# Sixteen-head attention: a cap applied by factors, work moved between four engines, a new slot table

## The reference

```
x = x + L0_attn(layernorm(x));  x = x + L0_moe(layernorm(x))      # before the stage of interest
q, k, v = split(layernorm(x) @ in_proj.T + in_proj_bias)           # 16 heads of 8
bias    = minimum((i - j) * slope[h], 8.0)                         # i query, j key; slope[h] = 2 ** (-0.5 (h+1))
scores  = q @ k.T * 8 ** -0.5 + bias
out     = softmax(scores) @ v                                      # per head
x = x + (out @ out_proj.T + out_proj_bias)
x = x + L1_ffn(layernorm(x))                                       # top-1 of 8 experts, after the stage
```

## Time and profile before

| | us |
|---|---|
| median of 3 runs | 988.6 |
| lowest, highest | 988.32, 989.9 |
| profiled execution | 988.53 |
| its span in the trace | 986.5 |

### The profile page before, as it was taken

The page is one execution under the profiler, slowest core; times in us unless marked ns, Lnnn a source line. Parts: engine busy times, 40 slices in busy tenths (PEclk is TensorE's granted clock), DMA queues, the critical chain, the costliest instruction groups (busy, mean ns, idle before and its releaser), DMA issues.

```text
span 986.5 us, 19021 instructions
## 1 busy us (share of the span) xinstructions
PE 783.2 (79%) x5641; PEld 564.8 (57%) x5641; DVE 549.3 (56%) x2190; ACT 395.9 (40%) x947; POOL 357.9 (36%) x543
## 2 busy tenths in 40 slices
PE   0798479999999999952489999999999982038894
PEld 0676355555666677742246676667666651028883
DVE  4688573233322332333588989898987714026672
ACT  0456121222212322210036666766676661025562
POOL 5000517777850134433222423242322102744552
PEclk9999668999999999986569999999999995559997
DMA  9970001111100132303654444444443014111110
GB/s 250 155 221 0 0 1 36 40 41 41 44 0 14 52 112 78 96 30 90 128 106 95 90 108 93 102 83 106 95 85 67 3 45 155 54 53 55 50 50 14
DMA packets 75114, 72.44 MB, mean 73 GB/s; under 512 B 8125, under 2 KB 65680, under 8 KB 72732
## 3 DMA queue, kind: packets, MB, share of 16 engines
q1 hardware_dynamic: 69436, 60.38, 27.3%
q0 software_dynamic: 5600, 11.12, 3.5%
HBM read 43.71 MB, written 27.33 MB: 72 GB/s over the span
## 4 chain that ended last, share of the span: by engine, by line
PE 52%; DVE 18%; issue 12%; DMA 5%; POOL 5%; ACT 3%; DVEq 2%; SPq 2%; POOLq 0%; ACTq 0%
PE bank L1475 10%; PE bank L1476 9%; DVE rt L1065 6%; PE bank L1498 6%; PE bank L1527 4%; PE bank L1617 3%; PE bank L1569 3%; POOL sorted_rows L766 3%; PE bank L1604 3%; PE bank L1599 2%; DMA arena<-arena 2%; SPq L548 1%; DVEq L1180 1%; PE bank L1435 1%; PE bank L1707 1%
## 5 line engine op out<-in xcount | busy, mean ns | idle before, releaser
L1065 DVE CUSTOM_DVE_ANT_0 rt<-bank,alibi 128x256 f32<-128x256 f32 x512 | 192.9, 419 | 44.4 <-PE bank L1569 37.5
L973 DVE TENSOR_TENSOR arena<-arena,bank 128x512 f32<-128x512 f32 (+1 forms) x128 | 75.0, 587 | 187.8 <-ACT arena L1253 187.8
L1280 ACT ACTIVATE arena<-bank 128x512 f32<-128x512 f32 x256 | 150.6, 598 | 55.4 <-PE bank L1604 49.5
L1253 ACT ACTIVATE arena<-bank 128x512 f32<-128x512 f32 (+1 forms) x128 | 66.1, 517 | 202.9 <-PE bank L1476 202.9
L1569 PE MATMUL bank<-arena 72*128 72x256 bf16 x512 | 104.7, 289 | 26.6 <-DMA arena<-qk_parts 13.4
L1599 PE MATMUL bank<-arena 81*128 81x256 bf16 x512 | 117.0, 274 | 8.3 <-ACT arena L1280 4.7
L1475 PE MATMUL bank<-arena 128*128 128x320 f32 (+2 forms) x256 | 115.7, 534 | 7.5 <-DVE arena L973 7.5
L1476 PE MATMUL bank<-arena 128*128 128x320 f32 (+2 forms) x256 | 111.9, 519 | 0.0
L1604 PE MATMUL bank<-arena,ident_b 128*128 128x256 bf16 (+8 forms) x544 | 80.2, 243 | 0.0
L1569 PEld LDWEIGHTS bank<-arena 72*128 72x128 bf16 x512 | 39.0, 102 | 69.4 <-DVE arena L1065 42.8
L1475 PEld LDWEIGHTS bank<-arena 128*128 128x128 f32 x256 | 42.8, 193 | 53.5 <-DVE arena L973 41.1
(11 more groups left out here) (242 smaller groups left out, 1402.9 us busy)
## 6 DMA issues: line engine op xcount, KB each, us to landing
arena<-qk_parts SPq DMA_DIRECT2D x48, 192.0 KB
arena<-qk_parts SPq DMA_DIRECT2D x144, 64.0 KB
qk_parts<-arena SPq DMA_DIRECT2D x16, 384.0 KB, 2.8
back_rows<-empty_row SPq DMA_DIRECT2D x1, 4096.0 KB, 37.8
arena<-back_rows SPq DMA_DIRECT2D x16, 256.0 KB, 3.8
arena<-in_w SPq DMA_DIRECT2D x2, 2048.0 KB, 10.9
xg_rows<-empty_row SPq DMA_DIRECT2D x1, 2580.0 KB, 38.5
arena<-xg_rows SPq DMA_DIRECT2D x8, 322.5 KB, 4.0
```

The costliest lines, as they stand in the source:

```text
L973: nc.vector.tensor_tensor(out, sil[:, k, 0:out.shape[1]], bank[4 + k][:, 0:out.shape[1]], ALU.mult).then_inc(hid_done, 1)
L1065: last = nc.vector.tensor_tensor_reduce(biased[n % 2 * QT + u], bank[n % 2][:, SEQ * u:SEQ * u + SEQ], alibi[:, h, P * (1 - u):P * (1 - u) ...
L1253: nc.scalar.activation(sil[:, k, 0:width], bank[2 + k][:, 0:width], ACT.Silu).then_inc(sil_done, 1)
L1280: nc.scalar.activation(prT3[:, n % (2 * HG)].rearrange("p k t -> p (k t)"), bank[2 + n % 2][:], ACT.Exp).then_inc(exp3_done, 1)
```

## The change

Heads 2 to 8 lose their cap matmuls. Only heads 0 and 1 (`FULL = 2`) keep the bias as matmuls on PE. For heads 2 to 8 the scores hold the uncapped bias, and after the exponential POOL multiplies the columns where the cap bites by exp(8 - slope * distance) (`apply_factor`); the factor table is made once. `weigh` waits for these products (`factored`), is split over two slots (`WEIGH_0`, `WEIGH_1`) and stands three slots later, with a ring of 12 heads for `prT3` and of 5 batches for `v3`. The third norm is applied by ACT (two instructions) instead of DVE, from a shift and a scale that POOL works out in four steps instead of one. ACT also copies the values, without bias; the value bias is multiplied by the output weights once, and added to the output bias. ACT issues the DMA of the maxima. The offsets of nearly all steps are new, and the projection of q and k stands one slot behind that of the values.

```diff
-FULL = 4
+FULL = 2
+PR = 3 * HG
+VRING = 5
-COMBINE_0, COMBINE_1, STATS, VARIANCE, NORM, TURN, HT, QKV, QK_COPY, VALUES = -41, -40, -39, -38, -33, -30, -29, -26, -25, -19
+COMBINE_0, COMBINE_1, STATS, VARIANCE, ROOT, NORM_0, NORM_1, OUTPUT_BIAS = -42, -41, -38, -37, -36, -34, -33, -29
+TURN, HT, VALUE, QK, Q_COPY, K_COPY, PARTS_QK, VALUES = -32, -31, -27, -26, -25, -24, -23, -21
+SPLIT_MAX_0, SPLIT_MAX_1, TURN_MAX, COPY_MAX, SEND_MAX = NH + 1, NH + 2, NH + 4, NH + 5, NH + 6
+FACTOR, WEIGH_0, WEIGH_1, KEEP = EXP_LAG + 2, EXP_LAG + 6, EXP_LAG + 7, EXP_LAG + 8
...
# SP
-        def send_max(c):
-            wait_apart(sp, (max_rows_done, c + 1))
-            sp.dma_start(qs[MROW:KALL, c % RING], max_rows[0:PARTS * NH, c % 2]).then_inc(max_in[c % 2], 16)
...
# POOL
+        def apply_factor(n):
+            c, h = divmod(n, NH)
+            pool.wait_ge(exp3_done, n + 1)
+            if n == FULL:
+                pool.wait_ge(factor_set, 1)
+            for k in range(QT):
+                first = capped_from(h, k)
+                if first < SEQ:
+                    pr = prT3[:, n % PR, k, first:SEQ]
+                    last = nc.gpsimd.tensor_tensor(pr, pr, factor[:, h - FULL, first - P * k:SEQ - P * k], ALU.mult)
+            last.then_inc(factored, 1)
...
# DVE
-            nc.vector.tensor_scalar(mv[:, p, :, 2], mv[:, p, :, 1], LN_EPS, None, ALU.add).then_inc(var3_done, 1)
-        def norm3(c):
-                last = nc.vector.tensor_scalar(h3[:, c % 2, u, :], x[:, 2 * c + u, :], mv[:, c % 2, u, 0:1], rstd3[:, c % 2, u:u + 1],
-        def values(c):
-                last = nc.vector.tensor_tensor(v3[:, c % RING, u, :, 0:HD], bank[6][:, SEQ + D * u:SEQ + D * u + D].rearrange("p (h d) -> p h d", d=HD),
...
# ACT
+        def normalise(c, u):
+            last = nc.scalar.activation(h3[:, c % 2, u, :], x[:, QT * c + u, :], ACT.Identity, scale=norm3[:, c % 2, u, 1:2],
+                                        bias=norm3[:, c % 2, u, 0:1])
+        def values(c):
+                last = nc.scalar.activation(v3[:, c % VRING, u, :, 0:HD],
+        def send_max(c):
+            wait_apart(act, (max_rows_done, c + 1))
+            act.dma_start(qs[MROW:KALL, c % RING], max_rows[0:PARTS * NH, c % 2]).then_inc(max_in[c % 2], 16)
...
# PE
-        def weigh(g):
+        def weigh(g, u):
+            if u == 0:
+                pe.wait_ge(exp3_done, HG * (g + 1))
+                if k * HG < CLAMPED:
+                    pe.wait_ge(factored, factors_to(HG * g + HG - 1))
```

More of the change, by code:

```diff
@@ L82, with capped_from, factors_to @@
 SLOPE_PARTS = [bf16_parts(s) for s in SLOPES]
[L83 to L89, removed]
+BIAS_PARTS = [len([v for v in SLOPE_PARTS[h] if v]) for h in range(FULL)]
+STRIP = [sum(BIAS_PARTS[:h]) for h in range(FULL)]
+FACTORS = CLAMPED - FULL
+def capped_from(h, k):
+    return min((P * k + int(MAX_BIAS / SLOPES[h]) + 1) // 2 * 2, SEQ)
+def factors_to(n):
+    c, h = divmod(n, NH)
+    return FACTORS * c + min(max(h + 1 - FULL, 0), FACTORS)
 def batch_at(slot, offset):
@@ L284, in _build @@
     strip_a = carve([P, sum(BIAS_PARTS[:FULL]), SEQ + P], BF16)
[L285 to L288, removed]
+    factor = carve([P, FACTORS, SEQ])
     q_row = carve([P, SEQ], BF16)
@@ L1292, in turned, with copy_q @@
             if c >= 1:
-                act.wait_ge(v3_mm, c)
+                act.wait_ge(qk3_mm, c)
             nc.scalar.activation(hT3, bank[6][:, 0:SEQ], ACT.Copy).then_inc(hT3_done, 1)
-        def copy_qk(c):
+        def values(c):
+            act.wait_ge(v3_mm, c + 1)
+            if c >= VRING:
+                act.wait_ge(pv3_mm, NH // HG * (c - VRING + 1))
+            for u in range(QT):
+                last = nc.scalar.activation(v3[:, c % VRING, u, :, 0:HD],
+                                            bank[6][:, SEQ + D * u:SEQ + D * u + D].rearrange("p (h d) -> p h d", d=HD), ACT.Copy)
+            last.then_inc(v3_done, 1)
+        def copy_q(c):
             act.wait_ge(qk3_mm, c + 1)
@@ L1461, in _ @@
         pe.wait_ge(w3_in, 128)
+        pe.wait_ge(bv_done, 1)
+        nc.tensor.matmul(bank[7][:, P:2 * P], bv_cols[:], w_out[:], start=True, stop=True)
         nc.tensor.matmul(bank[7][:, 0:E1], w_redT[:], wgT[:], start=True, stop=True).then_inc(gate_mm, 1)
@@ L1596, in score_turned @@
                 out = bank[2 + n % 2][:, SEQ * k:SEQ * k + SEQ]
-                first = bias_from(h, k) if h < CLAMPED else SEQ
-                biases = range(BIAS_PARTS[h]) if first < SEQ else ()
+                biases = range(BIAS_PARTS[h]) if h < FULL else ()
                 last = nc.tensor.matmul(out, ks[0:KALL, c % RING, h, P * k:P * k + P], qs[0:KALL, c % RING, h, :],
```

240 lines of the change are left out of this document (130 added, 110 removed).

## The result

The changed kernel is slower, not faster: 1019.5 us (median of four runs, 1014.8 to 1020.6) against 988.7 us before (988.3 to 989.9), a ratio of 1.028 with a 95% interval of 1.022 to 1.034; a fifth execution, which the ratio takes in, took 1008.2. The prediction was 957, its range 945 to 974. The profiled execution of the kernel after took 1014.8 us with a span of 1013.1.

What follows compares the result with a forecast made beforehand. PE was taken to bound the kernel, DVE close behind: 14.4 periods shortened from 19.6 to 17.6 us give 28.8, with 2 (start) and 1 (drain) 31.8, so 988.53 becomes 956.7, about 957 us; range 945 to 974.

Steps and rivals of the forecast that it cites:

- I take 3 us for it, by the row without queueing, so no wait: DMA of the maxima, issued from ACT: lands in about 3 us, so PE does not wait at head 0.
- that it stood behind twelve others in one queue: Argument against Slower: the 5.07 us of the maxima's DMA came from queueing on SP behind the DMAs of `replicate`.
- Slower: Rival, chance 0.05: maxima take as long from ACT as from SP, PE waits at head 0 of every batch; 1006 us.
- Period 17.6: Steady part of the second attention: one batch's period on PE falls from 19.6 to 17.6 us.
- ACT waits up to 1 us for `root5`: Fifth norm on ACT: POOL's `root5` ends near slot 20.3 but is wanted in 19, a wait up to 1 us.
- about one slot of slack before PE feels it: ACT's wait for `root5` was to stay hidden from PE by about one slot, slots being 1.1 us.
- POOL's products, 5.4 to 5.8: POOL's twelve new products over 1614 columns: 5.4 to 5.8 us per period, with PE not waiting for them.
- POOL decides: Rival, chance 0.12: products cost half as much again, those of heads 3 and 7 come late; period about 18.6, 972 us.
- DVE, ACT: Busy times per period: DVE falls from 17.7 to 15.9 us, ACT rises from 13.6 to 15.8.
- the "0.4": Allowance of 0.4 us per period for DVE's small instructions splitting the maxima, stalled beside POOL's products in slots 1 and 2.
- Start -2: Start of the stage: 2 us shorter, bounds -4 and +2, with the first maxima at 3 us instead of 6.11.
- Drain: End of the stage, 22.8 us: 1 us shorter, through up to 1.8 us fewer bias matmuls while ACT is busy.

Runs made afterwards that it cites:

- e1: The changed kernel with the DMA of the maxima issued from SyncE's queue again, behind the replication and ahead of the given rows: 1013.2 us, 1.026 of before.
- e5: The changed kernel, maxima still sent from ACT, with the given rows loaded only once the maxima have been sent: 1022.1 us, 1.029 of before.
- e2: The changed kernel with only 4 of the 12 replication reads issued from batch 4 on, so scores use old rows: 971.8 us, 0.981 of before.
- e7: e6 with both halves of a group product in one slot: 971.0 us, 0.974 of before.
- e12: The changed kernel, complete, replicating by two writes and six reads of 24 rows, with e7's two table shifts: 967.8 us, 0.973 of before.
- e6: e2 with the two instructions of the fifth norm on ACT three and two slots later: 974.9 us, 0.978 of before.
- e8: The changed kernel with the maxima sent from SyncE as three DMAs of one row each, sixteen heads apart: 1031.6 us, 1.030 of before.

## Why the prediction was wrong

The step that failed is **"I take 3 us for it, by the row without queueing, so no wait"**, for the DMA of the maxima. It took the duration of a DMA from a stretch without traffic and put it into one with twelve transfers under way. The argument against the rival Slower, "that it stood behind twelve others in one queue", was tested by e1 and e5: from either queue it lands at the end of the same traffic. The rows for the right answer were in the trace of before: landed 17.9 us behind the write of the parts, wanted 17.5 behind it. The forecast reckoned from the DMA's issue ("in slot 22, wanted in 25"), and neither the write nor the twelve reads, which the change moves later and the shorter slots squeeze, were counted as a chain with a deadline.

The rival Slower (chance 0.05) had the place and the direction. That its price of 1006 is near is partly luck: it had 16 waits of 3.1 us, 50 in sum, on a kernel of 957, where there were 26.7 us of waits, a low clock behind them, and a kernel of 972 without both. Its picture of "every batch" was off: even batches wait 2.3 to 4.7 us, odd ones 0 to 0.2. While PE waits, GpSimd's `parts` and the write of the next replication go on (POOL splits from 629.46, the write is issued at 633.67, PE goes on at 633.98), so the next one has a head start. The write and PE's wait of an odd batch show it:

```profile
593.97 0.38 SPq L536 DMA_DIRECT2D qk_parts<-arena  x1
...
611.56 0.28 PE L1651 MATMUL bank<-arena 81*128 81x256 bf16 x1 [0.17 <-DMA arena<-arena]
```

From this write to the wait's begin there are 17.4 us, where the even batches of the steady part have 13 to 13.6.

The other terms, read from the undisturbed periods and from e2, e7 and e12:

- **Period 17.6.** Undisturbed it is 17.97 after and 17.95 in e2; 17.5 in e6, e7 and the undisturbed batches of e12 (706.95 to 724.44). The gap of 0.4 is the place of the fifth norm, which e6 alone moves. The group product's halves cost little, 0.07 by e7 against e6, where the forecast had put 0.4.
- **ACT waits up to 1 us for `root5`.** It waits 1.6 to 1.9 us in the batches that don't follow a stop of PE, and "about one slot of slack before PE feels it" was too much: moving the fifth norm, which waits for it, takes the 0.4 off the period. In its timeline after:

```profile
623.43 0.49 ACT L1353 ACTIVATE arena<-xw 128x128 f32<-128x128 f32 x1 [1.61 <-POOL xw L738]
```

- **POOL's products, 5.4 to 5.8.** 84.1/16 = 5.26 us per batch, and PE never waited for one. The rival POOL decides falls with that.
- **DVE, ACT.** In the undisturbed period from 608.27 to 626.24 DVE is busy 16.2 us (15.9 forecast), POOL 12.1 (12.5), ACT 13.9 (15.8 with 0.7 for the issue, which isn't counted as busy; the rest was too high by 1.2). The combine's stall is gone but for single instructions of up to 0.70, some small stalls came where the "0.4" had them, the row maximum is untouched. All instructions of these lines (ns min/median/max; the first is the combine, to be set beside the 1.58 us for two in the earlier trace rows, the last the row maximum of the earlier trace rows):

```profile
L1048 DVE SCALAR_TENSOR_TENSOR xw<-arena,gate_w,xw x64: 319/347/700, 446.0 to 743.5; 128x128 f32<-128x128 f32 x64
L1088 DVE TENSOR_TENSOR arena<-arena x16: 191/194/492, 495.3 to 813.1; 128x32 f32<-128x32 f32 x16
L1076 DVE CUSTOM_DVE_ANT_0 rt<-bank,alibi x512: 393/420/427, 478.5 to 812.1; 128x256 f32<-128x256 f32 x171
```

- **Start -2.** Wrong in sign: +4 after, +6.8 in e2 (which still has the whole replication there). The first maxima took 8.75 us, not 3 (PE waits 4.25 for them at the start), behind the same replication.
- **Drain.** What follows the last projection is 5.2 us shorter in e2 (244.1 against 249.3), near the 1 + 2.6 x 2 forecast; after, it is +0.5, with a wait and a low clock in it.

With these sizes the sum is 988.5 + 6.8 - 11 x 1.65 - 5.2 = 972, which is e2 (971.8). The terms are read from e2 itself, so this only sorts its time and proves nothing. What it shows is the share of each error: 15 us of the miss of some 63 are mostly the start and the period, and 972 would still have been inside the range; the other 48 are the one step.

## What to carry to other kernels

A small transfer that must land by a slot isn't priced from its issue to its landing in a quiet stretch. Find the traffic it lands behind, measure the whole chain from the step that starts that traffic (16 to 18 us here, in both kernels), and hold it against the time between that step and the slot, in the new table and with the new, shorter slots. A tighter table cuts every such slack in proportion, and a step moved later cuts it by the move, so a list of the slacks belongs in the forecast beside the engines' sums. And where a wait goes along with a low clock, read stretch by stretch whether PE waits or works in it: here a filled wait gave nothing back while the traffic set the pace, and the low clock cost about 12 us in one stretch of full work.

## What was not expected of the hardware

- Six reads of 24 rows take about 9 us where three of 24 and nine of 8 take 15, at the same 1152 KB. The DMA share is the sign: in the 1-us stretches it is 0.43 to 0.54 in nine of fifteen with the twelve, 0.75 to 0.94 in six of nine with the six.
- The Trainium skill (DMA: Bandwidth & Descriptors, "Why a DMA increments its semaphore by 16 and not by 1") has a DMA from these queues go to the lowest-numbered k engines, k being the largest number up to 16 that divides the slowest dimension on both sides. By it reads of 8 rows use 8 engines and reads of 24 use 12, and the busiest carries 15 rows before and 12 in e12; the shares of half fit, the size of the gain doesn't follow from it (an estimate by this rule is 15 us x 12/15 = 12, about 9 was seen). By it the maxima's three rows go to three of the busiest engines; but e8, in which the same rule spreads each row over 16, gained nothing, so what they wait for isn't the choice of engines alone. That stays open.
- Issued from ScalarE (e5) or from SyncE (e1), the maxima landed at the end of the traffic both times: another queue was no way past it.
- Stops of 2.3 to 4.7 us brought the granted clock of after from 1.00 to 0.50, while the stops of up to 1.5 us in e12 did not. It could stay there for long: behind the stop that ends at 716.99 it is 0.50 until 747, 30 us in which PE has no wait.
